# One queue for all transfers, ten tile slots, half of the bias in PSUM, and three stores cut into 126 and 2 rows

## The reference

```
x0 = x
for wi, bi in zip(w, b):
    xw = x @ wi                 # one number for each row
    x  = x0 * xw + bi + x
```

## Time and profile before

| | |
|---|---|
| median of 3 runs | 1281.09 us (1280.54 to 1290.55) |
| profiled execution | 1280.2 us |
| its span | 1278.4 us |
| PE busy | 780.7 us (61%) |
| DVE busy | 1150.2 us (90%) |
| ACT busy | 102.7 us (8%) |
| moved | 537.28 MB, 420 GB/s over the span |
| mean granted PE clock | 0.782 |

### The profile page before, as it was taken

One profiled execution on the slowest core, in us unless ns is written; L12 is line 12 of the kernel. 1 busy time (PEld: TensorE's weight loads), 2 busy tenths in 40 slices (PEclk: granted clock), 3 DMA queues, 4 the chain that ended last, 5 costly groups with the idle time before them and its releaser, 6 DMA issues.

```text
span 1278.4 us, 20057 instructions
## 1 busy us (share of the span) xinstructions
PE 780.7 (61%) x9114; PEld 728.6 (57%) x9114; DVE 1150.2 (90%) x526; ACT 102.7 (8%) x345; POOL 4.3 (0%) x17
## 2 busy tenths in 40 slices
PE   8666666555656655556555665665655665665653
PEld 4666566555556655555545565565655654665653
DVE  5999999898988988989889898898998988989896
ACT  3000000000000000000000000000000000000010
POOL 1000000000000000000000000000000000000000
PEclk9877787887877778778787777777777778678677
DMA  9999999999999999999999999999999999999996
GB/s 385 416 380 428 430 431 431 429 427 429 433 429 431 431 430 432 430 431 424 421 424 425 418 427 421 424 425 422 427 424 421 424 423 425 425 423 425 426 421 286
DMA packets 37385, 537.28 MB, mean 420 GB/s; under 512 B 4168, under 2 KB 4168, under 8 KB 4728
## 3 DMA queue, kind: packets, MB, share of 16 engines
q1 hardware_dynamic: 18432, 268.44, 50.1%
q10 hardware_dynamic: 18936, 268.64, 49.3%
HBM read 268.63 MB, written 268.44 MB: 420 GB/s over the span
## 4 chain that ended last, share of the span: by engine, by line
DMA 72%; DVE 15%; PE 8%; issue 3%; ACT 1%; DVEq 0%
DMA out_dram<-tiles 56%; DMA tiles<-in_r_inputs_dram 15%; DVE tiles L286 8%; DVE blocks L264 7%; PE dots L401 6%; ACT spread L197 1%; PE dots L359 1%; PE scratch L339 1%; DMA tiles<-in_L_rec_w_dram 0%; PE strips L334 0%; PE strips L349 0%; ACT c_last L189 0%; PE turned L370 0%; DVE scale L275 0%; DVEq L42 0%
## 5 line engine op out<-in xcount | busy, mean ns | idle before, releaser
L401 PE MATMUL dots<-blocks,weights 128*64 128x128 f32 x7808 | 662.6, 349 | 380.8 <-DVE blocks L264 380.6
L401 PEld LDWEIGHTS dots<-blocks,weights 128*64 128x64 f32 x7808 | 628.7, 185 | 405.3 <-DVE blocks L264 405.2
L264 DVE STREAM_TRANSPOSE blocks<-tiles 128x2048 f32<-128x2048 f32 x256 | 576.0, 2288 | 100.1 <-issue 100.1
L286 DVE SCALAR_TENSOR_TENSOR tiles<-tiles,scale,c_last 128x4096 f32<-128x4096 f32 (+1 forms) x131 | 571.9, 4368 | 0.2
L197 ACT ACTIVATE spread<-dots,group_mask 128x128 f32<-128x128 f32 (+1 forms) x268 | 75.2, 363 | 1062.6 <-PE dots L401 1020.3
L370 PE MATMUL turned<-layer_sel,spread 128*128 128x8 f32 x512 | 68.1, 258 | 85.5 <-ACT spread L197 85.5
L370 PEld LDWEIGHTS turned<-layer_sel,spread 128*128 128x128 f32 x512 | 62.3, 191 | 101.4 <-issue 95.6
L359 PE MATMUL dots<-blocks,weights 128*64 128x64 f32 x768 | 32.4, 266 | 11.0 <-DVE blocks L264 11.0
L359 PEld LDWEIGHTS dots<-blocks,weights 128*64 128x64 f32 x768 | 31.7, 180 | 12.9 <-issue 12.9
L205 ACT ACTIVATE growth<-turned,ones 128x16 f32<-128x16 f32 (+1 forms) x67 | 18.3, 273 | 85.0 <-PE turned L370 85.0
L275 DVE TENSOR_TENSOR_SCAN scale<-growth,cw 128x6 f32<-128x6 f32 x128 | 13.3, 142 | 8.9 <-ACT growth L205 8.9
(11 more groups left out here) (25 smaller groups left out, 11.3 us busy)
## 6 DMA issues: line engine op xcount, KB each, us to landing
tiles<-in_r_inputs_dram SPq DMA_DIRECT2D x128, 2048.0 KB, 14.9
out_dram<-tiles ACTq DMA_DIRECT2D x127, 2048.0 KB, 25.5
out_dram<-tiles ACTq DMA_DIRECT2D x4, 512.0 KB, 7.0
tiles<-in_L_rec_w_dram ACTq DMA_DIRECT2D x1, 96.0 KB
tiles<-in_L_rec_b_dram ACTq DMA_DIRECT2D x1, 96.0 KB
```

Source lines behind the costliest of these rows:

```text
L264: nc.vector.transpose(blocks[:, p % PLACES, :], source).then_inc(blocks_ready, 1)
L286: nc.vector.scalar_tensor_tensor(out=tiles[:, s, at], in0=tiles[:, s, at], scalar=scale[:, u % 2, t, L - 1:L], in1=c_last[:, at], op0=ALU. ...
L401: last = nc.tensor.matmul(dots[at:at + KM * Q, :, :, :], weights[:, c * CH // Q + k:c * CH // Q + k + KM, :], place[:, :, k * Q:(k + KM) * Q],
```

## The change

The number of pairs of slots becomes `N_SLOTS` = 5, of two tiles each, so ten tile slots. `PLACES` becomes 2. All stores move from ACT's queue into SyncE's. SyncE issues store n, then waits until store n-3 (`LAG` = 3) has landed, then issues the load of tile n+7 into that slot. Tiles 0 to 7 and 9 are loaded at once, tile 8 after the preparation.

The stores of tiles 118, 121 and 124 go as two transfers, 126 rows and 2 rows.

The bias sum's second half stays in PSUM (`c_high` is `scratch` itself); the first half is copied to `c_low` in SBUF. A finish is now two instructions of 128 x 2048, one with each half. The sum of b is made from `b_rows`, loaded by four transfers of 6 rows, with `ones` as weights in four row groups of PE; `of_quarter` and `quarter_sum` go away. The strips of b stay for `cw`.

```diff
-PLACES = 4
+PLACES = 2
-N_SLOTS = 8
+N_SLOTS = 5
+LAG = 3
+MOST = 126
+IN_TWO = (118, 121, 124)
...
+            for n in range(TB * LAST_PAIR_OF_PREP):
+                load(n)
+            load(TB * LAST_PAIR_OF_PREP + 1)
+            sp.wait_ge(weights_ready, G)
+            sp.wait_ge(bias_summed, 2)
+            sp.wait_ge(strips_summed, 1)
+            load(TB * LAST_PAIR_OF_PREP)
+            def store(n):
+                q, s, t = place_of(n)
+                sp.wait_ge(tiles_done, n + 1)
+                if n in IN_TWO:
+                    sp.dma_start(out_pairs[q, 0:MOST, t, :], tiles[0:MOST, s, t, :]).then_inc(y_stored[s][t], 16)
+                    sp.dma_start(out_pairs[q, MOST:P, t, :], tiles[MOST:P, s, t, :]).then_inc(y_stored[s][t], 16)
+                else:
+                    sp.dma_start(out_pairs[q, :, t, :], tiles[:, s, t, :]).then_inc(y_stored[s][t], 16)
+
+            for n in range(n_tiles - 1):
+                store(n)
+                into = n - LAG + TB * N_SLOTS
+                if TB * N_SLOTS <= into < n_tiles:
+                    q, s, t = place_of(into)
+                    sp.wait_ge(y_stored[s][t], 16 * (q // N_SLOTS))
+                    load(into)
...
             act.dma_start(strips_w, w_strips).then_inc(w_landed, 16)
-            act.dma_start(strips_b, b_strips).then_inc(b_landed, 16)
-
-            act.wait_ge(ones_ready, 1)
-            act.wait_ge(of_quarter_ready, 1)
             for j in range(G):
-                nc.scalar.activation(quarter_sum[:, j, :], ones[:], ACT.Copy,
-                                     scale=of_quarter[:, j:j + 1]).then_inc(quarter_sum_ready, 1)
+                act.dma_start(b_rows[j * Q:j * Q + L, :, :], b_halves[j]).then_inc(b_landed[j], 16)
+            act.dma_start(strips_b, b_strips).then_inc(strips_b_landed, 16)
...
+            act.wait_ge(bias_summed, 1)
+            nc.scalar.copy(c_low[:], c_high).then_inc(c_low_ready, 1)
...
-            keep_bias(0)
-            spread_dots(0)
-            keep_bias(1)
             act.wait_ge(cw_all_ready, 1)
             nc.scalar.copy(cw[:], strips[:, 0, 0:LP]).then_inc(cw_ready, 1)
+            spread_dots(0)
             make_growth(0)
             for u in range(1, n_units):
-                first, n_of = tiles_of(u - 1)
-                if tiles_of(u)[1] == 1:
-                    spread_dots(u)
-                    make_growth(u)
-                    for t in range(n_of):
-                        store(first + t)
-                else:
-                    store(first)
-                    spread_dots(u)
-                    for t in range(1, n_of):
-                        store(first + t)
-                    make_growth(u)
...
+                spread_dots(u)
+                make_growth(u)
...
-                parts = 1 if n < n_tiles - 1 else PIECES
+                parts = 2 if n < n_tiles - 1 else STORE_PARTS
                 width = D // parts
                 for i in range(parts):
                     at = slice(i * width, (i + 1) * width)
-                    nc.vector.scalar_tensor_tensor(out=tiles[:, s, at], in0=tiles[:, s, at],
-                                                   scalar=scale[:, u % 2, t, L - 1:L], in1=c_last[:, at],
-                                                   op0=ALU.mult, op1=ALU.add).then_inc(tiles_done, 1)
+                    c = c_low[:, at] if i < parts // 2 else c_high[:, i * width - HALF:(i + 1) * width - HALF]
+                    done = nc.vector.scalar_tensor_tensor(out=tile[:, at], in0=tile[:, at],
+                                                          scalar=scale[:, u % 2, t, L - 1:L], in1=c,
+                                                          op0=ALU.mult, op1=ALU.add)
+                    if parts == STORE_PARTS or i == parts - 1:
+                        done.then_inc(tiles_done, 1)
...
             def sum_bias(h):
                 for j in range(G):
-                    last = nc.tensor.matmul(scratch[:, j, :], quarter_sum[0:STRIPS, j, :],
-                                            strips_b[:, h * BANK:(h + 1) * BANK], start=True, stop=True)
-                last.then_inc(scratch_filled, 1)
+                    if h == 0:
+                        pe.wait_ge(b_landed[j], 16)
+                    last = nc.tensor.matmul(scratch[:, j, :], ones[j * Q:j * Q + L, :], b_rows[j * Q:j * Q + L, h, :],
+                                            start=True, stop=True, tile_position=(j * Q, 0))
+                last.then_inc(bias_summed, 1)
```

More of the change, by code:

```diff
@@ L34, in cross_network @@
     W_BANKS = SW // BANK
-    PW = D // PIECES
-    assert L <= LP and G * LP == Q and n_tiles % N_SLOTS == 0 and HEAD == TB and HEAD + n_pairs * TB + TAIL == n_tiles
-    assert STRIPS <= Q and SW == W_BANKS * BANK and W_BANKS == 2
+    HALF = D // 2
+    assert L <= LP and G * LP == Q and HEAD == TB and HEAD + n_pairs * TB + TAIL == n_tiles
+    assert STRIPS <= Q and SW == W_BANKS * BANK and W_BANKS == 2 and HALF == G * BANK and TAIL // TB < N_SLOTS
+    x_pairs = x.rearrange("(q t p) d -> q p t d", p=P, t=TB)
+    out_pairs = out.rearrange("(q t p) d -> q p t d", p=P, t=TB)
     w_strips = w.rearrange("l (j n) a -> (l j) (n a)", j=G)
     b_strips = b.rearrange("l (j n) -> (l j) n", j=G)
+    b_halves = b.rearrange("l (h j n) -> j l h n", h=2, j=G)
     with ExitStack() as ctx:
@@ L132, in _, with load @@
         def _(sp):
[L133 to L142, removed]
+            def load(n):
+                q, s, t = place_of(n)
+                sp.dma_start(tiles[:, s, t, :], x_pairs[q, :, t, :]).then_inc(x_landed[s][t], 16)
@@ new lines, in _ @@
+            for n in range(n_tiles - 1):
[5 more added lines that the diff above has]
+                    load(into)
+            q, s, t = place_of(n_tiles - 1)
+            for i in range(STORE_PARTS):
+                at = slice(i * D // STORE_PARTS, (i + 1) * D // STORE_PARTS)
+                sp.wait_ge(tiles_done, n_tiles + i)
+                sp.dma_start(out_pairs[q, :, t, at], tiles[:, s, t, at]).then_inc(y_stored[s][t], 16)
@@ L144, in _ @@
+            for n in range(n_tiles - TB * N_SLOTS, n_tiles):
+                q, s, t = place_of(n)
+                last_stores = STORE_PARTS if n == n_tiles - 1 else 2 if n in IN_TWO else 1
+                sp.wait_ge(y_stored[s][t], 16 * (q // N_SLOTS + last_stores))
         @block.gpsimd
@@ L202, in make_growth @@
                 act.wait_ge(turned_ready, u + 1)
-                if u > 0:
+                if u == 0:
+                    act.wait_ge(ones_ready, 1)
+                else:
                     act.wait_ge(scale_ready, first)
@@ L256, in transpose_pieces @@
                 first, n_of = tiles_of(u)
-                s = first % N_SLOTS
+                s = first // TB % N_SLOTS
                 for c in pieces:
@@ L261, in transpose_pieces @@
                         dve.wait_ge(blocks_used, p - PLACES + 1)
-                    source = tiles[:, s, c * PIECE:(c + 1) * PIECE] if n_of == 1 else \
-                        tiles[:, s:s + TB, c * CH:(c + 1) * CH]
+                    source = tiles[:, s, first % TB, c * PIECE:(c + 1) * PIECE] if n_of == 1 else \
+                        tiles[:, s, :, c * CH:(c + 1) * CH]
                     nc.vector.transpose(blocks[:, p % PLACES, :], source).then_inc(blocks_ready, 1)
@@ L268, in wait_tiles @@
                 for n in range(first, first + n_of):
-                    dve.wait_ge(x_landed[n % N_SLOTS], (n // N_SLOTS + 1) * 16)
+                    q, s, t = place_of(n)
+                    dve.wait_ge(x_landed[s][t], 16 * (q // N_SLOTS + 1))
             def scan(u):
-                first, n_of = tiles_of(u)
+                n_of = tiles_of(u)[1]
                 dve.wait_ge(growth_ready, u + 1)
@@ L279, in finish @@
                 n = tiles_of(u)[0] + t
-                s = n % N_SLOTS
+                tile = tiles[:, n // TB % N_SLOTS, n % TB, :]
                 dve.wait_ge(scale_ready, n + 1)
-                parts = 1 if n < n_tiles - 1 else PIECES
+                parts = 2 if n < n_tiles - 1 else STORE_PARTS
                 width = D // parts
@@ L395, in _ @@
                 pe.wait_ge(dots_spread, n * G + (HEAD - 1) * G)
-                for c in range(PLACES):
-                    pe.wait_ge(blocks_ready, n * PLACES + c + 1)
-                    place = blocks[:, c, :].rearrange("p (t n) -> p t n", t=TB)
+                for c in range(PIECES_OF_PAIR):
+                    pe.wait_ge(blocks_ready, n * PIECES_OF_PAIR + c + 1)
+                    place = blocks[:, c % PLACES, :].rearrange("p (t n) -> p t n", t=TB)
                     for k in range(0, CH // Q, KM):
@@ L404, in _ @@
                                                 start=(c == 0 and k < parts * KM),
-                                                stop=(c == PLACES - 1 and k >= CH // Q - parts * KM),
+                                                stop=(c == PIECES_OF_PAIR - 1 and k >= CH // Q - parts * KM),
```

64 lines of the change are left out of this document (26 added, 38 removed).

## The result

The changed kernel is slower: 1287.88 us in the median of 20 runs (1280.93 to 1295.38) against 1280.74 us for the kernel before (20 runs, 1278.78 to 1292.67). The ratio is 1.0055, with a 95% interval of 1.0041 to 1.0069. The profiled execution took 1285.4 us, its span 1283.7 us. One execution of a later kernel, the halves by columns, took 2784.08 us and is left out of that kernel's ratio.

What follows compares the result with a forecast made beforehand. One late DMA engine, 9.91 us per tile, was taken as the bound. With it spared, T at 1202.4 plus 71.0 us of second chain gave 1273.4, span -5.0, so 1276 us in the median, -0.4%; range 1262 to 1289.

Steps and rivals of the forecast that it cites:

- What bounds the kernel: Whole kernel: one late DMA engine, at 9.91 us per tile, sets the pace; the other engines take 9.74.
- Ten slots, queue, PSUM half, places: Middle and tail: slots gain 0, SyncE stores -0.5 us, PSUM half 0.19 us per tile (tail +1.4), places hidden.
- Order at the end: Last loads: with one queue L(123) comes right behind S(116), so T moves by -2.5 us, to 1202.4.
- T: Tail: the time tile 123 has landed and DVE starts tiles 122 and 123; 1204.9 us before, forecast 1202.4.
- D: Rival, whole kernel: lateness comes from alternating two queues, so the pace becomes 9.74 us per tile, 1255 us; chance 0.14.
- Head: Start: first finish 1 us earlier, 4 us of idle queue near 67 us; sum 0, between -2 and +3.
- Rows 126 and 2: Last stores: two engines spared three stores, 14.9 us; pays only if the late one is spared, two in three.
- Case B: Rival, end: the late engine is not spared and ends at 1280.4 us, giving 1283 us; chance 0.22.
- theory M: Experiments' theory, cut stores: engines moving rows outside their group hold each other up, 3 us or more; no chance given.
- The tail's second chain: End: DVE's work on the last tiles, last finish 65.5 us after T, ends the kernel once the late engine is spared.
- C: Rival, one queue: one direction at a time costs 2.4% per packet, 28.6 us, 1305 us; chance 0.12.

Runs made afterwards that it cites:

- the halves by columns: Kernel before with the stores of tiles 118, 121 and 124 cut in two by columns, 128 rows by 2048 each: 1281.94 us against 1281.07, ratio 1.0002.
- probes: Changed kernel without splits (1298.87, 1297.43 us) and kernel before (1282.77 us), some stores in three parts, first of few rows, its landing marked by GpSimd.
- The two-queue experiment: Changed kernel without the splits and with stores back in ACT's queue, in the kernel before's order: 1280.16 us against 1281.15, ratio 0.999.

## Why the prediction was wrong

**What bounds the kernel: right.** One late engine sets the pace in the kernel before and in the changed one. Its surplus was read rightly from the even load issues against the rate of the windows, and the completions and probes show it.

**Ten slots, queue, PSUM half, places: worth nothing together, as forecast.** The finish cost 0.21 us per tile for 0.19. With ten slots the others ran ahead for 1000 us instead of 600 (431 GB/s in both windows after), and the late engine gained nothing by it. DVE's wait for block places came to 3.8 us over the whole span. The two-queue experiment bears these parts out together (0.999), and one queue without the split is within its interval of the kernel before.

**Order at the end: near the mark by luck.** T was forecast 2.5 us earlier, because of the one queue, and came 3.2 us earlier. But T in the kernel with one queue and no split, then in the one with two queues:

```profile
1205.14 4.50 DVE L269 STREAM_TRANSPOSE blocks<-tiles 128x2048 f32<-128x2048 f32 x2 [2.42 <-issue]
...
1200.07 4.50 DVE L269 STREAM_TRANSPOSE blocks<-tiles 128x2048 f32<-128x2048 f32 x2 [1.75 <-issue]
```

One queue alone did not bring T forward in its profile, and two queues with ten slots did, by 4.8 us, with no gain at the end (T + 78.3). So the reason given for the 2.5 us is not borne out.

**The pace in one queue: a small part of D, and lost again.** Load issues in the kernel before, in the changed kernel, and at the end of the one without the split:

```profile
L142 SPq DMA_DIRECT2D tiles<-in_r_inputs_dram x71: 327/328/328, 308.3 to 1002.0; - x71
...
L145 SPq DMA_DIRECT2D tiles<-in_r_inputs_dram x61: 339/473/602, 300.3 to 892.5; - x61
...
L147 SPq DMA_DIRECT2D tiles<-in_r_inputs_dram x13: 431/432/536, 1080.4 to 1203.1; - x13
```

They are 693.7/70 = 9.91, 592.2/60 = 9.87 and 122.7/12 = 10.2 us apart. The prediction had 9.91 or 9.74. In the middle one queue gained 0.04 us per tile, and the kernel without the split lost it again over its last loads. The cause of neither is known.

**Head: nothing, as forecast, but the idle dip hardly came.** From 68 to 70 us the DMA share was 0.35 before; after, where a dip of about 4 us was forecast near 67 us, it was 0.89.

```profile
68.00:70.00 2.00, 1.05 (x8) 0.97 (x8) 2.00 (x2) 0.45 (x2) 0.00 (x0) 1.00 0.35 147
...
68.00:70.00 2.00, 1.05 (x8) 0.97 (x8) 2.00 (x2) 0.78 (x4) 0.00 (x0) 0.94 0.89 377
```

**Rows 126 and 2: wrong, in two ways.** This is the step that failed.
1. "It pays only if the late engine is one of the two spared" was given two in three. It is the fifth, and it took nine rows each time. Case B, which had 0.22, was this case. The views could not name the engine, so two in sixteen was the honest chance from rows. The Trainium skill, DMA: Bandwidth & Descriptors, "Latency and other measured facts", calls engines 7 and 15 usually slower, counted from 0. The probes differ: with 5 and 6 rows one engine is late, which with 4 it is not, so the measurement decides against that rule here. The divisor rule of the same page, "Why a DMA increments its semaphore by 16 and not by 1", agrees with the trace: 14 and 2 completions.
2. The price of a miss was put at 2 to 4 us, as three or six packets more. B's sum was 1283; the median is 1287.9. The term left out is what such a store does to every engine. Cut by rows into 64 and 64, with no row more on any engine, three stores cost 1.1%, 14 us, about 5 each. Cut by columns they cost 0.02%. So it is the cut by rows that costs, and not the number of transfers. That it costs because engines then move other rows than in a store of 128 is theory M's reason; no run shows which engine moved which row.

In the profile of the changed kernel the late engine ended at T + 82. B had T + 78, with 1.9 for three packets. In the profile without the split it ended at T + 76.6, which B without its packets, T + 76.1, foresaw well. The 4 us that B lacks are put down to this second term; since T itself differs by 3.5 us between the two profiles, the size is not shown by them.

The whole of the change's loss can be the split's as far as the intervals tell: 1.0055 with it, 1.0006 without. How much of the rest (0.9982 to 1.0029) is the one queue's is open.

**The tail's second chain: right, and without effect.** The last finish ended 64.9 us after T and the fifteen engines at about T + 70.5, so the span would have ended near 1273, an estimate, had the late engine been spared for nothing. The one way of sparing it that was tried, 124 and 4 rows, cost more than it gave.

**C and D: neither in the main.** One direction at a time did not slow the middle (431 GB/s), and the lateness did not go away with one queue (9.87 us per tile, not 9.74).

## What to carry to other kernels

When the DMA engines are the bound, look for one late engine before adding slots: evenly spaced issues that are slower than the rate the engines reach together, a lone engine (a share of 1/16) at the end, and one completion of each store long after the rest. Keep large transfers at 128 rows, as their neighbours have. A cut by columns was free here. A cut by rows cost some 5 us for each 2 MB store near the end, also when it gave every engine the same work, and less in the middle. To take load from one engine, first find out by a probe which engine it is, and count what the others take over against their lead.

## What the runs showed of the hardware

- One DMA engine of sixteen, the fifth in the order in which parts of few rows take them up, was late in every probed kernel and on three chips. In the kernel before with the probe it came 13 us after the four before it, at 956 us. Why it is slower is not settled.
- While stores of 64, 124 or 126 rows ran among stores of 128, packets of 611 ns in the median took up to twice that and more (142 over 1.15 us after 1190 us with three stores of 64 and 64 rows, 2 in the kernel before), while the DMA share stays near 1. That engines then meet at the same memory port is a guess that fits; it was not tried by itself. In the kernel before three stores cut into 4 or 5, 12 or 11, and 112 rows in the middle cost under 2 us in one run. With one queue eight and six such stores came out 14 to 16 us above the kernel without them, some 2 us each, in one run each. So the price seems to depend on when it falls: this is open too.
- Kernels with a single queue spread more from run to run: 1276.01 to 1291.05 in twelve runs against 1278.65 to 1283.14 in eleven with two queues. The kernel before is mostly as close, with 1290.55 and 1292.67 as exceptions in twenty runs. The cause was not looked for.
- A VectorE finish over 128 x 2048 with one operand in PSUM took 2341 ns, with that operand in SBUF 2332 ns.
